# An attention and mixture-of-experts kernel: extra TensorE products in every free step, a shorter modulation stage, and block 1's stores on other queues

## The reference

```python
mod = (silu(c) @ wmod).reshape(B, 6, 1, -1)
sa, ca, ga, sb, cb, gb = (mod[:, i] for i in range(6))
ga = (2 * (ga >= 0) - 1) * maximum(abs(ga), 0.25)      # the gates; gb the same
gb = (2 * (gb >= 0) - 1) * maximum(abs(gb), 0.25)
h = layernorm(x) * (1 + ca) + sa
x = x + ga * attention(h)
h = layernorm(x) * (1 + cb) + sb
x = x + gb * moe(h)                                    # top 2 of 8 experts

# attention: q, k, v of h; causal, all in f32
scores = alpha * tanh(q @ k.T / beta) + lam * hamming + lattice   # both biases bilinear in tanh codes of h
out = softmax(scores) @ v @ out_w.T
```

## Time and profile before

| | us |
|---|---|
| three runs, median (lowest to highest) | 2020.63 (2010.03 to 2028.41) |
| profiled execution, its own time | 2022.98 |
| its span in the trace | 2021.2 |
| mean granted TensorE clock of it | 0.926 |

### The profile page before, as it was taken

One profiled execution on the slowest core, in us unless ns is written; L12 is line 12 of the kernel. 1 busy time (PEld: TensorE's weight loads), 2 busy tenths in 40 slices (PEclk: granted clock), 3 DMA queues, 4 the chain that ended last, 5 costly groups with the idle time before them and its releaser, 6 DMA issues. The chain is left out here.

```text
span 2021.2 us, 33603 instructions
## 1 busy us (share of the span) xinstructions
PE 1811.4 (90%) x10688; PEld 1076.5 (53%) x10689; DVE 1209.0 (60%) x2539; ACT 1233.8 (61%) x1292; POOL 512.2 (25%) x535
## 2 busy tenths in 40 slices
PE   2868999999999979999999997689559999999997
PEld 1333333333334333333333334568459999999997
DVE  7446768878778757778777775867313333333332
ACT  1157889989989968999999993234213333333332
POOL 0535331331232333411000001405612222222222
PEclk7768879989989979999999998889779999999999
DMA  4489674564562477754844404631366666666663
GB/s 152 122 215 187 157 149 102 118 121 110 121 126 70 114 186 147 138 124 108 191 76 76 87 6 133 203 122 69 110 204 182 182 180 175 186 181 181 176 183 79
DMA packets 186101, 280.29 MB, mean 139 GB/s; under 512 B 18512, under 2 KB 120784, under 8 KB 183824
## 3 DMA queue, kind: packets, MB, share of 16 engines
q1 hardware_dynamic: 172272, 259.94, 51.1%
q0 software_dynamic: 13440, 17.97, 4.5%
q10 hardware_dynamic: 288, 1.08, 0.2%
HBM read 213.90 MB, written 65.03 MB: 138 GB/s over the span
## 5 line engine op out<-in xcount | busy, mean ns | idle before, releaser
L963 DVE SCALAR_TENSOR_TENSOR probs<-probs,scal,bil_ps 128x512 f32<-128x512 f32 (+1 forms) x1152 | 788.2, 715 | 286.2 <-PE bil_ps L817 233.5
L896 ACT ACTIVATE probs<-probs 128x2048 f32<-128x2048 f32 (+1 forms) x288 | 522.7, 1815 | 101.5 <-DVE probs L963 101.0
L889 ACT ACTIVATE probs<-raw_ps 128x2048 f32<-128x2048 f32 (+1 forms) x288 | 508.9, 1767 | 28.9 <-PE raw_ps L800 28.4
L817 PE MATMUL bil_ps<-u_mv,w_st 50*128 50x512 f32 (+3 forms) x1280 | 470.9, 469 | 38.0 <-DVE probs L963 33.5
L817 PEld LDWEIGHTS bil_ps<-u_mv,w_st 50*128 50x128 f32 x1280 | 196.3, 192 | 528.9 <-DVE probs L963 448.6
L1635 ACT ACTIVATE hid_t<-fc_ps,b 128x128 f32<-128x128 f32 x576 | 156.3, 382 | 403.4 <-PE fc_ps L1602 236.0
L836 PE MATMUL o_ps<-probs,v_sb 128*32 128x512 f32 (+3 forms) x2560 | 314.5, 575 | 19.4 <-POOL probs L714 13.2
L800 PE MATMUL raw_ps<-q_mv,k_st 64*128 64x512 f32 (+3 forms) x1280 | 270.8, 406 | 15.2 <-DMA q_mv<-q_split 9.5
L1602 PE MATMUL fc_ps<-rows_t,w 128*128 128x128 f32 x2304 | 270.5, 276 | 0.0
L1602 PEld LDWEIGHTS fc_ps<-rows_t,w 128*128 128x128 f32 x2304 | 264.6, 193 | 0.1
L1613 PE MATMUL fc_ps<-w,hid_t 128*128 x1152 | 260.5, 379 | 0.0
(11 more groups left out here) (213 smaller groups left out, 1356.9 us busy)
## 6 DMA issues: line engine op xcount, KB each, us to landing
w<-in_w SPq DMA_DIRECT2D x80, 1024.0 KB, 6.0
q_mv<-q_split SPq DMA_DIRECT2D x128, 128.0 KB, 7.6
k_st<-k_split SPq DMA_DIRECT2D x48, 256.0 KB, 8.5
rows<-x_rows SPq DMA_DIRECT2D x72, 130.0 KB, 2.2
v_rows<-rows_sb SPq DMA_DIRECT2D x8, 1024.0 KB, 7.7
o_t<-o_sb SPq DMA_DIRECT2D x32, 256.0 KB, 9.4
k_st<-k_split SPq DMA_DIRECT2D x16, 512.0 KB, 8.6
v_sb<-v_rows SPq DMA_DIRECT2D x8, 1024.0 KB, 13.6
```

The costliest lines, as they stand in the source:

```text
L817: mm = pe.matmul(bil_ps[:, hd % 2, column:column + width], w_st[row:row + BIAS_ROWS, b, kt * P:(kt + 1) * P], u_mv[row:row + BIAS_ROWS, p, ...
L889: act.activation(probs[:, s % NBUF, :, first:BLK], raw_ps[:, :, first:BLK], ACT.Tanh).then_inc(tanh_ready, 1)
L896: act.activation(scores, scores, ACT.Exp).then_inc(exp_ready, 1)
L963: dve.scalar_tensor_tensor(scores, scores, scal[:, ALPHA:ALPHA + 1], bil_ps[:, hd % 2, first:BLK], ALU.mult, ALU.add).then_inc(sum_ready, 1)
```

## The change

Three things change. (1) `FILL_AT` holds every step without a part, 173 in place of 111. After a C, the extra product writes rows 64 to 127 of the bank only and doesn't wait for the code to be read. (2) In the modulation, the gate chain goes: VectorE moves parts 0, 1, 4 and 5 of each batch, ScalarE copies parts 2 and 3 together; the gates are finished by four instructions on 128x4x256 at the start of the output stage. The first loads of the front stage are issued at the end of the modulation's SP stream, so their tiles and semaphores are made outside both stages. In the first diff hunk of the modulation the lines left out load wcode, wqkv, head_sum and soft_sum; in the vector one they are the five instructions of the gate chain. (3) Block 0's key stores and block 1's query and key stores are issued by ScalarE, after its `high_half`s of that block; the other stores of block 1 are issued by SP in step 0 of the loop, behind the key and bias loads of iteration 2. Part 4 of a batch is a scale (1.0 is added), part 5 a gate, part 3 a shift.

```diff
@@ FILL_AT
-        if half != 0 and s >= last + (3 if o == "C" else 2):
-            FILL_AT[s] = (i, o)
+        assert half != 0
+        FILL_AT[s] = (i, o)
@@ stage_modulation, sync
+            for i in range(EARLY):
+                row = BLOCKS[i][0] * T + BLOCKS[i][1] * BLK
+                sp.dma_start(x_blk[:, i, :, :], ...).then_inc(xb_in[i], 16)
+                if i == 0:
...
@@ stage_modulation, scalar
+            act.wait_ge(mod_done, 1)
+            for b in range(B):
+                cols = slice((b * 6 + 2) * D, (b * 6 + 4) * D)
+                act.activation(modrow[:, cols], mod_ps[:, cols], ACT.Copy)
@@ stage_modulation, vector
-                    if part % 3 == 0:
+                    if part % 3 == 1:
+                        dve.tensor_scalar(modrow[:, cols], mod_ps[:, cols], 1.0, None, ALU.add)
+                    elif part in (0, 5):
                         dve.tensor_copy(modrow[:, cols], mod_ps[:, cols])
-                    elif part % 3 == 1:
-                        dve.tensor_scalar(modrow[:, cols], mod_ps[:, cols], 1.0, None, ALU.add)
-                    else:
...
@@ stage_front, sync
-            load_rows(0)
...
-            load_rows(1)
-            for o in ("Q0", "C", "Q1", "Q2", "L", "Q3"):
+            for o in ("Q0", "Q1", "C", "L"):
                 store(0, o)
...
-            for o in ("Q0", "C", "Q1", "Q2", "L", "Q3", "V1"):
-                store(1, o)
             load_rows(3)
             for s in range(NSTEP):
...
                 if s in BIAS_AT:
                     load_bias(BIAS_AT[s])
+                if s == 0:
+                    for o in ("C", "L", "V1"):
+                        store(1, o)
@@ keep_clock
                 if o == "C":
-                    pe.wait_ge(code_ready, i + 1)
+                    pe.matmul(part_ps[ROWS:P, :], ident[:, ROWS:P], modrow[:, 0:BLK], start=True, stop=True)
                 else:
                     pe.wait_ge(emptied, EMPTIED[i, o])
-                pe.matmul(part_ps[:, :], ident[:, :], modrow[:, 0:BLK], start=True, stop=True)
+                    pe.matmul(part_ps[:, :], ident[:, :], modrow[:, 0:BLK], start=True, stop=True)
@@ stage_front, scalar, for blocks i = 0 and 1
                 for m in range(4):
                     high_half(i, m)
+                for m in ((2, 3), range(4))[i]:
+                    act.wait_ge(emptied, EMPTIED[i, f"Q{m}"])
+                    store_heads(act, i, m)
@@ stage_output, vector
             dve.memset(blank[:, :], 0.0).then_inc(blank_ready, 1)
+            gates = modrow[:, :].rearrange("p (g s d) -> p g s d", s=3, d=D)[:, :, 2, :]
+            dve.scalar_tensor_tensor(gate_abs[:, :, :], gates, -1.0, gates, ALU.mult, ALU.max).then_inc(gate_step, 1)
+            dve.tensor_scalar(gate_sign[:, :, :], gates, 0.0, 2.0, ALU.is_ge, ALU.mult)
+            dve.wait_ge(gate_step, 1)
+            dve.tensor_scalar(gate_abs[:, :, :], gate_abs[:, :, :], 0.25, None, ALU.max).then_inc(gate_step, 1)
+            dve.wait_ge(gate_step, 2)
+            dve.scalar_tensor_tensor(gates, gate_sign[:, :, :], -1.0, gate_abs[:, :, :], ALU.add, ALU.mult
+                                     ).then_inc(gate_step, 1)
+            dve.wait_ge(gate_step, 3)
```

More of the change, by code:

```diff
@@ L173, in build @@
             lattice = c2.enter_context(nc.sbuf_tensor("lattice", [HEX, H * HEX], F32))
-            stage_modulation(nc, a, modrow, ident, scal, shift, rstd, lattice)
-            stage_front(nc, a, dram, modrow, ident, scal, shift, rstd, lattice, rows_sb, x_back)
+            head_sum = c2.enter_context(nc.sbuf_tensor("head_sum", [H * HEX, H], F32))
+            soft_sum = c2.enter_context(nc.sbuf_tensor("soft_sum", [HROWS, H], F32))
+            p_in = c2.enter_context(nc.semaphore("p_in"))
+            x_in = [c2.enter_context(nc.semaphore(f"xb_in{p}")) for p in range(2)]
+            front = (head_sum, soft_sum, p_in, x_in)
+            stage_modulation(nc, a, modrow, ident, scal, shift, rstd, lattice, rows_sb, front)
+            stage_front(nc, a, dram, modrow, ident, scal, shift, rstd, lattice, rows_sb, x_back, front)
         sb = lambda scope, n, shape, dt=F32: scope.enter_context(nc.sbuf_tensor(n, shape, dt))
@@ L212, with borrowed, borrow, stage_modulation @@
 HAM, SCALE, ALPHA, BETA, SIG_HAM, SIG_SCALE, HALF_LAM, LAT_SCALE, INV_BETA, ROOM = range(10)
-def stage_modulation(nc, a, modrow, ident, scal, shift, rstd, lattice):
+def borrowed(rows_sb):
+    used = [0]
+    def borrow(n):
+        used[0] += n
+        return rows_sb[:, used[0] - n:used[0]]
+    wqkv = borrow(KC * 3 * D).rearrange("p (k n) -> p k n", k=KC)
+    wcode = borrow(KC * HROWS).rearrange("p (k n) -> p k n", k=KC)
+    x_blk = borrow(2 * TPB * D).rearrange("p (q t d) -> p q t d", q=2, t=TPB)
+    xn = borrow(2 * D).rearrange("p (q d) -> p q d", q=2)
+    h = borrow(TPB * D).rearrange("p (t d) -> p t d", t=TPB)
+    h_t = borrow(KC * BLK).rearrange("p (k t) -> p k t", k=KC)
+    v_st = borrow(TPB * H * VW).rearrange("p (t h v) -> p t h v", t=TPB, h=H)
+    return wqkv, wcode, x_blk, xn, h, h_t, v_st
+def stage_modulation(nc, a, modrow, ident, scal, shift, rstd, lattice, rows_sb, front):
     with ExitStack() as ctx:
@@ L260, in _ @@
                 load_x(sp, q)
+            head_sum, soft_sum, p_in, xb_in = front
+            wqkv, wcode, x_blk = borrowed(rows_sb)[:3]
+            for i in range(EARLY):
+                row = BLOCKS[i][0] * T + BLOCKS[i][1] * BLK
+                sp.dma_start(x_blk[:, i, :, :], a["x"][row:row + BLK, :].rearrange("(t p) d -> p t d", p=P)
+                             ).then_inc(xb_in[i], 16)
+                if i == 0:
+                    sp.dma_start(wcode[:, :, :], a["code_wt"].rearrange("(k p) n -> p k n", p=P)).then_inc(p_in, 16)
+                    sp.dma_start(wqkv[:, :, :], a["qkv_wt"].rearrange("(k p) n -> p k n", p=P)).then_inc(p_in, 16)
+                    sp.dma_start(head_sum[:, :], a["head_sum"]).then_inc(p_in, 16)
+                    sp.dma_start(soft_sum[:, :], a["soft_sum"]).then_inc(p_in, 16)
         @block.scalar
@@ L378, in stage_front @@
         o_sb = sb("o_sb", [P, 2, BLK])
[L380 to L393, removed]
+        head_sum, soft_sum, p_in, x_in = front
+        wqkv, wcode, x_blk, xn, h, h_t, v_st = borrowed(rows_sb)
         qk_f = sb("qk_f", [P, BLK])
@@ L415, in stage_front @@
         part_ps = ps("part_ps", [P, BLK])
-        p_in, pad_ready, ones_ready = sem("p_in"), sem("pad_ready"), sem("ones_ready")
-        x_in = [sem(f"xb_in{p}") for p in range(2)]
+        pad_ready, ones_ready = sem("pad_ready"), sem("ones_ready")
         h_ready, part_mm, emptied, code_ready, hi_ready = (
@@ L464, in part_rows, with store_heads @@
             return view[b:b + 1, side, part, :, c * BLK:(c + 1) * BLK].rearrange("z h r t -> (z h) r t")
+        def store_heads(eng, i, m):
+            b, c = BLOCKS[i]
+            for part, src in enumerate((qk_hi, qk_lo)):
+                eng.dma_start(part_rows("q_split" if m < 2 else "k_split", H, 2, HD,
+                                        slice((m % 2) * 8, (m % 2) * 8 + 8), part, b, c),
+                              src[:, m, :].bitcast(F32)).then_inc(st_qk[m], 16)
         def normalise(eng, then_wait, i, t):
@@ L507, in store @@
                         sp.wait_ge(lo_ready, 4 * (i - EARLY) + m + 1)
[L508 to L511, removed]
+                    store_heads(sp, i, m)
                 elif o == "L":
@@ L1022, in stage_output @@
         gated = sb("gated", [P, D])
+        gate_abs = sb("gate_abs", [P, B * 2, D])
+        gate_sign = sb("gate_sign", [P, B * 2, D])
+        gate_step = sem("gate_step")
         bn = sb("bn2", [P, NTILE * 6])
```

18 lines of the change are left out of this document (1 added, 17 removed).

## The result

| | before | after |
|---|---|---|
| median of 4 runs each, us (lowest to highest) | 2020.55 (2010.03 to 2028.41) | 1996.47 (1991.92 to 1997.15) |
| profiled execution, its own time | 2022.98 | 1991.92 |
| its span | 2021.2 | 1990.2 |

The ratio is 0.9879, with a 95% interval of 0.9832 to 0.9927: 24 us less, where 47 were forecast. A second set of runs of the same kernel gave 0.9877 (0.9846 to 0.9908).

What follows compares the result with a forecast made beforehand. ScalarE was taken to pace the loop at 3.634 us a step, with TensorE just fitting at full clock but pacing where it dips. Savings 29 + 8.5 + 3.9 + 6 = 47.4 us, 2020.63 to 1973 us; range 1956 to 1997.

Steps and rivals of the forecast that it cites:

- rival B: Attention loop: the clock's dips are not for want of products; 18.4 us saved, 2002 us; chance 0.11.
- rival A: Loop's start: DMA engines bind it, so moved stores give -3 us instead of 6; 1982 us; chance 0.20.
- Extra products: Attention loop: a product in all free steps, 62 added, keeps TensorE's clock up; 29 us saved.
- the 119 steps: Loop steps 24 to 143: about 436 us forecast from 458.6; over 450 would make the forecast wrong.
- the term of 29 us: Loop: nine tenths of 26.1 + 6.0 = 32.1 us over the 3.634 us pace of the last stretch.
- at the full clock one is free: Loop: an extra product costs a step almost nothing, 3.68 us with one against 3.58 without.
- Modulation: Ahead of the loop: VectorE drops the gate chains and ScalarE copies parts 2 and 3; 8.5 us saved.
- First loads: Ahead of the loop: rows and weights are there at the barrier, so normalising starts earlier; 3.9 us saved.
- Stores of block 1: Loop's start: TensorE's 9.48 us wait for iteration 2's keys goes, less a late tanh; 6 us saved, bounds -3 and 12.
- Middle stretch and gates: Loop from 682 to 760 us, and gates finished in the output stage: 0 taken for each.
- C: Loop's start and middle stretch: more comes back, a third of the rest, 13 us; 1960 us; chance 0.13.
- D: Loop up to step 206: TensorE lacks reserve, 61 products cost 1.12 us each, 68 us; 2041 us; chance 0.04.

Runs made afterwards that it cites:

- x1: The kernel before with extra products in all 173 free steps and nothing else of the change: ratio 0.9932 (0.9908 to 0.9955).
- x5: The changed kernel without the extra products of steps 32, 33, 72 and 73: one run, 2000.8 us.
- x2: The kernel before with the shorter modulation, earlier first loads and gates in the output stage alone: ratio 0.9927 (0.9906 to 0.9949).
- x3: The kernel before with block 1's stores moved (heads to ScalarE's queue, others behind iteration 2's loads) alone: ratio 0.999 (0.9975 to 1.0005).
- x6: The changed kernel with Pool's splitting of the codes in two pieces, so a mask can run between: ratio 0.9838 (0.9782 to 0.9894).
- x7: The changed kernel with extra products up to step 207 on 256 columns in place of 512: ratio 0.985 (0.979 to 0.9909).
- x10: x9 with the extra products up to step 207 on 256 columns, as in x7: ratio 0.9786 (0.9734 to 0.9837) to the kernel before.
- x4: The changed kernel with block 1's query and key stores given back to SP, behind its other stores in step 0: ratio 0.9878 (0.985 to 0.9905).
- x8: The changed kernel with 1 MB of x more copied into unused DRAM, ahead of the keys of iteration 1: one run, 1997.4 us.
- x9: x6 with an iteration's values loaded ahead of the next bias rows on SP's queue: ratio 0.982 (0.9772 to 0.9868) to the kernel before.
- x11: The changed kernel again, unaltered, against the kernel before: ratio 0.9877 (0.9846 to 0.9908).

## Why the prediction was right and wrong

The direction is right, and so are two of the three mechanisms, the products that hold the clock and the shorter head. The third, the moved stores, brought nothing. The time lies in the range, but at its edge (1996.5, with 1997 as the upper bound), and the saving is half of the forecast's. By the time alone rival B (2002) was nearer than the forecast (1973), and rival A (1982) too; that the products work is known from x1 and from the stretches, not from the time. By its steps:

- **Extra products.** The mechanism is right (x1, x5): the 119 steps took 445.1 us, where 436 were forecast and over 450 would have been the sign of a wrong one. The step that failed is the term of 29 us: x1 gives 13.8 by ratio. The stretches of the two profiles give 13.5 + 3.5 = 17.0, but part of that is luck of the profile before. First, the 26.1 us that this profile showed over the pace are one draw: x2 and x3, whose loop has the same products as before, were 453.3 - 432.5 = 20.8 and 453.8 - 432.5 = 21.3 us over, and with the stretch 160 to 207 there were some 28 us to win, not 32.1. Second, 12.6 + 2.5 = 15.1 us were still over the pace afterwards, where I had allowed for 3.1. Not all of it was the clock. Steps 114 and 115 take 13.6 us in the changed kernel, 6.4 over the pace, since a mask waits behind Pool's splitting and the clock is low behind this wait; I put all that the stretch was over to the clock from its DMA share, and didn't look at Pool. x6 takes them away. Third, "at the full clock one is free" was read from one pair of steps. In a run of steps that all have a product or a part, TensorE has no reserve, and about one step in five takes 3.9 us; x7 and x10 put 3.3 and 4.2 us on this in the stretch 24 to 143. The last stretch, from which I took the pace, has no parts for VectorE to read. x10, with both taken away, is 2.3 + 0.9 us over the pace in the two stretches.
- **Modulation.** Taken as 8.5, right: VectorE ended its move at 29.63, for 38.94, and 0.8 us of these 9.3 come from the statistics before it, which ended earlier.
- **First loads.** Taken as 3.9, right: normalising starts 0.3 us behind the end of the move, for 4.4 before. Together 43.35 - 29.95 = 13.4 us, and x2 shows that all of it reaches the end (15 us by ratio, 14.5 at step 12). The first tanh came 12.9 us earlier, not 9 to 10; the excess is mainly the clock ahead of the loop, luck of the two profiles.
- **Stores of block 1.** Taken as +6, this failed: step 12 starts 15.6 us earlier, of which x2 has 14.5 alone, and x3 alone gains nothing. The wait for the keys of iteration 2 went as forecast, but its time came back. TensorE waits 4.6 us for the keys of iteration 1 (2.3 in x1 and 2.6 in x2, which don't move the stores) and 3.0 us for the values of iteration 3 (3.1 in x3, under 0.8 in x1 and x2). The mask's 4.3 us in step 9 are not the stores' doing: x1 and x2 have them as well, and the kernel before has 3.3. The late tanh was 5.4 to 5.7 us instead of 3.2, because an issue on ScalarE took 1.1 us and not 0.73. Why is open: with all issues on SP they took 1.4 us each (x4). Rival A had the size right (-3 to +1). Its reason is shown in part: 1 MB more early on costs nothing (x8), but later, around 140 to 153, a transfer is slow, as the values show that land 13.5 to 14.4 us after their issue, early or late (x6, x9). That the DMA engines are the limit there is the likely reading and was not tried by itself. For it speaks their busy share there (1.05, under x9). The Trainium skill's rule (Trainium Kernel Development and Optimization, Key Constraints), that a second queue saves only the issue time, agrees with x3 and x4, where moving the stores gave nothing that the ratio can show.
- **Middle stretch and gates.** Taken as 0, measured +0.6; the gates took 1201.72 to 1205.34, and VectorE still waited 1.59 us for TensorE behind them.
- **Rivals.** B fell with x1 and x5. C fell: nothing came back in the middle, and the start gave less than forecast. D didn't happen as a whole, but a small share of its mechanism did, the 3 to 4 us above.

The parts taken alone add up to more than the whole: 13.8 (x1), 14.8 (x2) and 2 (x3), 30.6 us by ratio, for 24.4 together. Their intervals are wide enough for the 6 us between, so it is not shown that the parts get in each other's way.

Left open: which step of the loop's start paces it when the stores are moved, since each order ends at step 12 within 161 to 165 us (168 with block 1's heads on SP); what makes one issue take 0.6 us and the next 1.8; why the clock is low at steps 27 and 41, and for longer ahead of the loop, in some executions, with no product missing; and why the part behind the loop took 9 us longer in the set of x9 to x11.

## What to carry to other kernels

Extra products that hold TensorE's clock are worth their place only up to what the clock needs: try half the size, because a free step is also the reserve in which a slower step is caught up. Where a stretch takes longer than its pace, name what each long step waits for (clock, mask or transfer) before it is put down to one cause, and take the size of a thing that moves from run to run from more than one profile, before and after. A wait that goes from a chain of loads comes back at the next load, unless the whole chain is shorter.

## What the runs showed of the hardware that was not expected

- An issue's time varies by three times, and not for a second queue alone: eight stores took 0.58 to 2.03 us each on ScalarE's queue while SP issued too, and the same eight 0.63 to 1.80 us on SP's while ScalarE issued nothing (x4). Three key loads took 1.24 to 3.93 us on SP in the kernel before.
- The clock's dips depend on the execution: in steps 24 to 143 the same loop was 20.8 to 26.1 us over its pace in three profiles, and with the whole products in and the splitting as before, 12.5 to 14.2 in four of five profiles and 19.3 in the other (x8).
- The granted clock of a short stretch and the products agree: in the kernel before it is 1.00 up to 417 us, 0.50 from 419 to 427 and 1.00 from 429, and the products of the earlier trace rows take 1.93 us at 419.44 and 1.06 at 429.79.
- A value load took 13.5 to 14.4 us from issue to landing in a stretch where the DMA engines are busy all the time, for 10.0 in the median, and moving its issue 1.3 us forward didn't bring it earlier.
- Halving the columns of an extra product took it from 1.12 to 0.70 us, and the granted clock stayed at 0.99 and 1.00 (x7).
